# Five of 128 adjacency loads issued as 120 and 8 partitions in a graph-attention kernel

## The reference

```python
def _L0_gnn_ref(x, adj, W, a):
    h = x @ W
    s_src = h @ a[:F_out, 0]
    s_dst = h @ a[F_out:, 0]
    e = jax.nn.leaky_relu(s_src[:, None] + s_dst[None, :], negative_slope=0.2)
    e = jnp.where(adj > 0, e, NEG_INF)
    return jax.nn.softmax(e, axis=1) @ h

h = jnp.maximum(_layernorm(x, axis=-1), 0.0)
x = x + _L0_gnn_ref(h, adj, W, a)
```

## Time and profile before

| | before |
|---|---|
| median of the runs | 862.4 us (856.88 to 864.73) |
| span of the profiled execution | 813.7 us |
| median less span | 48.7 us |
| busiest engines, share of the span | DVE 73%, ACT 66%, PE 63%, POOL 62% |
| DMA, mean over the span | 368 GB/s |
| data of the main DMA queue | 276.83 MB |

### The profile page before, as it was taken

The page is one execution under the profiler, slowest core; times in us unless marked ns, Lnnn a source line. Parts: engine busy times, 40 slices in busy tenths (PEclk is TensorE's granted clock), DMA queues, the critical chain, the costliest instruction groups (busy, mean ns, idle before and its releaser), DMA issues.

```text
span 813.7 us, 8992 instructions
## 1 busy us (share of the span) xinstructions
PE 510.1 (63%) x1855; PEld 228.0 (28%) x1855; DVE 592.3 (73%) x3117; ACT 534.2 (66%) x375; POOL 508.1 (62%) x522
## 2 busy tenths in 40 slices
PE   3686666665766576766655676676666575666421
PEld 3552222222222232322222232222322132222121
DVE  7916477766776768777779668777786787768984
ACT  3999676676767667676766767677676666676300
POOL 3643776655666665577666656656777655567771
PEclk9899657677666766776687656657676767677655
DMA  9989999999999999999999999999999999998110
GB/s 335 418 298 407 403 404 410 408 411 408 407 408 412 410 408 407 411 405 404 396 401 409 391 410 396 392 409 396 399 401 392 395 384 365 402 401 320 40 30 11
DMA packets 43239, 299.31 MB, mean 368 GB/s; under 512 B 11468, under 2 KB 18290, under 8 KB 26800
## 3 DMA queue, kind: packets, MB, share of 16 engines
q1 hardware_dynamic: 25312, 276.83, 84.3%
q0 software_dynamic: 15328, 17.58, 6.9%
q10 hardware_dynamic: 2544, 4.33, 1.6%
HBM read 304.31 MB, written 8.65 MB: 385 GB/s over the span
## 4 chain that ended last, share of the span: by engine, by line
DMA 69%; ACT 12%; issue 8%; DVE 6%; PE 3%; SPq 0%; POOLq 0%; ACTq 0%; DVEq 0%
DMA adj_buf<-in_adj 69%; ACT mask_buf L465 10%; DVE x_all L806 2%; PE banks L1034 2%; ACT work L429 1%; PE banks L1003 1%; ACT prob L479 0%; ACT gathered L444 0%; ACT work L439 0%; SPq L264 0%; PE banks L1075 0%; PE banks L993 0%; DVE rest L623 0%; DVE words L625 0%; DVE w_x L874 0%
## 5 line engine op out<-in xcount | busy, mean ns | idle before, releaser
L465 ACT ACTIVATE mask_buf<-adj_buf,minus_half 128x2048 bf16<-128x2048 int32 x256 | 501.1, 1994 | 215.8 <-DMA adj_buf<-in_adj 215.4
L358 POOL DMA_INDIRECT gathered<-table,index x448 | 448.3, 1001 | 249.8 <-issue 150.9
L1034 PE MATMUL banks<-mask_buf,bit_ident 128*128 128x512 bf16 x1024 | 383.1, 521 | 114.1 <-ACT mask_buf L465 113.0
L1034 PEld LDWEIGHTS banks<-mask_buf,bit_ident 128*128 128x128 bf16 x1024 | 106.2, 123 | 335.4 <-ACT mask_buf L465 201.4
L806 DVE SCALAR_TENSOR_TENSOR x_all<-gathered,weight,x_all 128x128 f32<-128x128 f32 x512 | 157.7, 348 | 7.3
L621 DVE MAX8 words<-banks 128x8 f32<-128x512 f32 x64 | 44.8, 699 | 142.5 <-PE banks L1034 142.4
L1032 PE MATMUL banks<-key_rows,ones_b 3*128 3x512 bf16 x64 | 32.2, 503 | 126.2 <-ACT mask_buf L465 125.7
L1075 PE MATMUL banks<-x_all,one_hot 128*128 128x128 f32 x128 | 44.5, 450 | 17.8 <-DVE x_all L806 17.8
L1032 PEld LDWEIGHTS banks<-key_rows,ones_b 3*128 3x128 bf16 x64 | 6.1, 95 | 155.5 <-ACT mask_buf L465 154.4
L625 DVE MAX8 words<-rest 128x8 f32<-128x512 f32 x64 | 44.5, 695 | 2.2
L1075 PEld LDWEIGHTS banks<-x_all,one_hot 128*128 128x128 f32 x128 | 36.9, 324 | 27.7 <-DVE x_all L806 19.0
(11 more groups left out here) (160 smaller groups left out, 521.0 us busy)
## 6 DMA issues: line engine op xcount, KB each, us to landing
adj_buf<-in_adj SPq DMA_DIRECT2D x128, 2048.0 KB, 19.0
gathered<-table,index POOLq DMA_INDIRECT x448, 6.4
table<-gathered ACTq DMA_DIRECT2D x4, 1040.0 KB, 8.2
out<-x_all SPq DMA_DIRECT2D x31, 128.0 KB, 19.0
x_all<-in_x SPq DMA_DIRECT2D x3, 1024.0 KB, 10.5
x_all<-in_x SPq DMA_DIRECT2D x2, 512.0 KB, 5.2
w_gathered<-table,w_index POOLq DMA_INDIRECT x24, 5.9
out<-x_all SPq DMA_DIRECT2D x2, 64.0 KB
```

The costliest lines, as they stand in the source:

```text
L358: nc.gpsimd.indirect_dma_start(g_cols[buf][:, k, :], None, table, bass.IndirectOffsetOnAxis(index[:, buf, k:k + 1], 0), bounds_check=N, oo ...
L465: nc.scalar.activation(mask_buf[:, u], adj_buf[:, u], ACT.Sign, bias=minus_half[:]).then_inc(mask_ready, 1)
L1034: ins = mm(bank, bit_ident[:, h * PART_BITS + c], mask_buf[:, u, c * BIT_COLS:(c + 1) * BIT_COLS], start=False, stop=(h == PARTS - 1 and c ...
```

## The change

Five loads, those into place `u = 2` of batches 3, 9, 15, 21 and 27, are issued as two DMAs: the first 120 partitions of the same 2 MB, and then the last 8. Both raise the semaphore of the place by 16, so that place counts one more DMA from that batch on. `landed(i, u)` gives the count that ScalarE's mask waits for: for units 2 and 3 it is 16 times the number of DMAs issued into the place so far, for all others it is `16 * (i + 1)` as before. What is loaded, where to, and what waits for it is the same.

```diff
+SPLIT_UNIT = 2
+SPLIT_BATCHES = (3, 9, 15, 21, 27)
+SPLIT_AT = 120
...
+        def landed(i, u):
+
+            splits = sum(1 for j in SPLIT_BATCHES if j <= i) if u // 2 == SPLIT_UNIT // 2 else 0
+            return 16 * (i + 1 + splits)
...
             def load_two(i, u):
                 source = rows_of(adj, i * BATCH + u // PARTS, 1)[:, 0, u % PARTS * PART:(u % PARTS + 2) * PART]
-                sp.dma_start(adj_buf[:, u:u + 2, :].rearrange("p u n -> p (u n)"), source).then_inc(adj_loaded[u // 2], 16)
+                place = adj_buf[:, u:u + 2, :].rearrange("p u n -> p (u n)")
+                if u == SPLIT_UNIT and i in SPLIT_BATCHES:
+                    sp.dma_start(place[0:SPLIT_AT], source[0:SPLIT_AT]).then_inc(adj_loaded[u // 2], 16)
+                    sp.dma_start(place[SPLIT_AT:P], source[SPLIT_AT:P]).then_inc(adj_loaded[u // 2], 16)
+                else:
+                    sp.dma_start(place, source).then_inc(adj_loaded[u // 2], 16)
...
             def mask(i, u):
-                act.wait_ge(adj_loaded[u // 2], 16 * (i + 1))
+                act.wait_ge(adj_loaded[u // 2], landed(i, u))
```

## The result

The changed kernel took 894.22 us (median of 4 runs, 890.88 to 896.65), the kernel before 862.19 us in the same comparison: a ratio of 1.0374, interval [1.0336, 1.0411], **32.0 us slower**. The forecast was 866 us, and its range ended at 889.

A forecast was written before the change was run, and what follows sets the result against it. The prediction took the 16 DMA engines as the bound. Issue 0, Bytes 3.2 and Completion 0 summed to +3.2 us, added to the median of 862.4 us for 865.6, say 866 us; range 847 to 889.

The forecast's parts named there:

- Bytes: DMA engines at the five split loads: the fullest engine carries 9 rows in place of 8, adding 3.2 us.
- slower: Engines' write into the buffer: split loads run at half rate, up to 28.5 us more, 891 us; chance 0.36.
- faster: Split loads: one lagging DMA engine is left without a row, giving 849 us, 834 at most; chance 0.24.
- Issue: SP queue: five more DMAs cost 1.6 us of issue, hidden behind queued loads, so 0 is added.
- Completion: ScalarE's mask waiting for two pieces: 0 added; 20.5 us if each piece added a round trip.
- What bounds the kernel: Whole kernel: the 16 DMA engines set the pace, 69% of the chain of waits, 5.7 us per load.

The follow-up runs named there:

- e7: Changed kernel with the five loads cut into eight DMAs of 16 neighbouring partitions each: 893.34 us, 1.0558 of the kernel before.
- e4: Changed kernel with the second piece left out, so the five loads bring only 120 partitions: 880.36 us, 1.0423 of the kernel before.
- e1: Changed kernel with the five loads cut by columns, two DMAs of 128 partitions and half rows: 861.85 us, 0.9996 of the kernel before.
- e8: Changed kernel with the five loads as two DMAs, 64 even and 64 odd partitions: 849.02 us, 0.9956 of the kernel before.
- e10: Changed kernel with the five loads as four DMAs of every fourth partition: 861.91 us, 1.0007 of the kernel before.
- e11: Changed kernel with the five loads as eight DMAs of 128 partitions, an eighth of each row: 860.62 us, 1.0002 of the kernel before.

## Why the prediction was wrong

**The failed step is *Bytes*.** It took 0.64 us for a row of 16 KB from whole loads and gave it to the rows of any piece. While a split load is moved a row takes 1.17 us on average. The step counted how many rows the fullest engine gets (9 in place of 8, 3.2 us); 64 + 64 can be dealt out evenly and is slower all the same (883.89 us), and 10.6 to 12.6 us are lost per split load where the step's own upper bound is 5.1. So the count was not the question. What decides is which partitions are moved in one DMA: even and odd free, every fourth free, whole columns free; 64, 112 or 120 neighbours, 16 neighbours and every eighth not.

**The rival *slower* had the effect; its mechanism is argued, not shown.** It put the place at the engines' write into the buffer, two engines at one place and half the rate, and asked for dips at the split loads with ScalarE's longest waits there. The dips are at all five places; at the last one, as at the third, the kernel before is low as well, but with idle engines. The waits view (us in total, times, longest us) has ScalarE's waits for a load, kernel before (863.3 us), then changed:

```profile
ACT mask_buf L465 <- DMA adj_buf<-in_adj: 56.8, 39, 2.7
```

```profile
ACT mask_buf L478 <- DMA adj_buf<-in_adj: 130.0, 50, 8.6
```

The longest went from 2.7 to 8.6 us. All of more than 6 us end between 115 and 720 us, each at most 34 us behind one of the five split pairs (issued at 87.6, 232.3, 382.0, 536.1 and 687.0 us). A little more than half the rate is what the dip shows, 225 against 405 GB/s. Its price was off twice, in opposite senses: 5.7 us per load, but the loads in flight beside it are slowed too and 10.6 to 12.6 us are lost; and all of it on the end, while some 19 us fall into idle time of the DMA engines and 20.8 us are taken back behind the last load. 891 us against 894.22 is thus nearer than its working deserves. Its own doubt, that engines out of step collide less, may be what spoiled the fourfold slowing of e7; that wasn't shown.

Here the rule that the prediction weighed as a rival can be tested. The Trainium skill ("SBUF — State Buffer", section "Door 1: The DMA port swizzle") gives 16 ports by bits 2 to 4 and bit 6 of the partition number. By that formula even or odd partitions reach all 16 ports, every fourth all 16, every eighth 8, 64 neighbours 8, 16 neighbours 4. The runs agree where they are sorted: 16 ports 849.02, 861.91 and 860.62 us, at the level of the kernel before in their comparisons; fewer, 877.57 to 893.34 us and dips. They do not follow it in size: 4 ports (893.34 us) cost no more than the change. And 112 or 120 neighbours reach all 16 ports too, and yet are slow. So what the prediction drew from this rule, that the time is the rival's, does not come out of it for the long piece, which alone makes the run 880.36 us. For a whole load, the skill's "DMA: Bandwidth & Descriptors" (section "The descriptor swizzle") says that each engine writes one port of its own; that a piece of 120 is dealt out otherwise, several engines to one port, would close the gap, but no view here shows an engine's partitions, so this last link is argued and not shown.

**The rival *faster*** did not show: no run that may leave engines without rows is quicker than the kernel before (e4, 120 alone, 1.0423). Whether one engine lags is open, since the slower rows would cover such a gain.

***Issue*** held, and ***Completion*** for pieces of at least 32 partitions: one more DMA per load costs nothing in e1 and e8, three more nothing in e10, seven more nothing in e11. For the piece of 8 partitions *Completion* took 0, and it adds 2.6 us; how much of that is slow rows and how much completion was not separated. The prediction also cited the Trainium skill ("DMA: Bandwidth & Descriptors", section "Rules for kernel authors") for two transfers to disjoint parts running through the same engines; the page says of two partition halves that they serialize. The runs agree with that for even and odd partitions (0.9956); for two ranges of 64 it says too little, since they take longer (1.0282) than the same bytes in one DMA.

**The frame was wrong too.** The prediction took the 48.7 us between median and span for time around the span; 1.8 us lie there. It read an execution in which loads set the pace until 700 us and called it the kernel. In the execution of 863.3 us DMA holds 2% of the chain that ended last, in place of 69%, and VectorE 71%: the step *What bounds the kernel* does not hold there. A gap of 5.6% (48.7 of 862.4 us) between the profiled span and the median should have been read as a sign that the trace is not of a usual execution. This did not change the direction, but the prediction's sentence that there is no slack to absorb a slower load "until 600 us" is not true of such executions.

## What to carry to other kernels

In this kernel the rate of a DMA into the buffer depends on which partitions it covers, even at equal bytes and rows: cut a large load by columns, or by every second or fourth partition, and not by ranges of partitions. A few per cent fewer partitions, 120 in place of 128, were enough to bring the rate down to 225 GB/s from 405, and the transfers beside it are slowed with it. The DMA share does not show this, since slow rows are busy rows: divide bytes by the busy time, or read GB/s by time. And before a trace is taken for the kernel, compare its span with the times of other executions.

## What was not expected of the hardware

- A piece of 8 partitions with 128 KB costs 2.6 us of the end, (893.2 - 880.36) / 5, while a store of the same size lies unseen among the loads.
- Rows of 2 KB in place of 16 KB cost nothing in five 128-partition loads (1.0002): 30352 packets on the main queue where the changed kernel has 25347, and 413 GB/s from 237 to 260 us.
- Sixteen neighbours at a time dip to 208 GB/s where 120 + 8 dip to 272, and yet the whole takes the same 893 us. Why is open.
- The kernel before has executions of quite different pace: a span of 813.7 us with the DMA engines full until 700 us, and one of 863.3 us in which they miss 33 us between 100 us and the last load, and the end hangs on VectorE. The runs of the kernels with dips were all between 876 and 898 us, except the one with 31 splits.
